# Layer 2's experts: W1 of a slot placed ahead of W2 of the slot before, experts visited in ascending order of tokens, two weight buffers for all of them, and the first slot placed among the sort's matmuls

## The reference, cut to what matters

```python
leaf = zeros(N)
for d in range(4):                       # 16 leaves
    logits = xf @ Wr[off:off+cnt].T + br[off:off+cnt]
    sel = take(logits, leaf);  leaf = leaf * 2 + (sel > 0)
for e in range(16):                      # only the rows of leaf e count
    h = gelu(xf @ W1[e] + b1[e])         # 512 -> 2048
    y = h @ W2[e] + b2[e]                # 2048 -> 512
    out += onehot(leaf)[:, e] * y
x = x + out
```

## Time and profile before

| what | us |
|---|---|
| median of three runs (lowest, highest) | 1835.92 (1829.23, 1841.54) |
| the profiled execution, span; no other time of it is given | 1832.5 |
| PE matmuls busy in the span | 1658.9 (91%) |
| DVE busy | 850.0 (46%) |
| ACT busy | 472.2 (26%) |
| POOL busy | 128.8 (7%) |
| mean granted TensorE clock | 0.942 of full |

### The profile page before, as it was taken

One profiled execution on the slowest core, in us unless ns is written; L12 is line 12 of the kernel. 1 busy time (PEld: TensorE's weight loads), 2 busy tenths in 40 slices (PEclk: granted clock), 3 DMA queues, 4 the chain that ended last, 5 costly groups with the idle time before them and its releaser, 6 DMA issues. The chain is left out here.

```text
span 1832.5 us, 26087 instructions
## 1 busy us (share of the span) xinstructions
PE 1658.9 (91%) x8767; PEld 1029.9 (56%) x8768; DVE 850.0 (46%) x2173; ACT 472.2 (26%) x928; POOL 128.8 (7%) x193
## 2 busy tenths in 40 slices
PE   6889889999999999898999999998899988799964
PEld 3345564476457589896576766656334433464532
DVE  6665376821266674523733426534233322513464
ACT  2012224430020132221636116411223321231220
POOL 0011000000000003431100000001000000200000
PEclk9798999999999899898999989998999989899996
DMA  5131126200071078863000102045998784230000
GB/s 157 63 117 34 43 84 235 80 12 0 10 295 35 25 283 261 272 185 90 4 23 24 72 32 80 1 184 193 427 429 359 300 372 189 83 105 1 0 1 28
DMA packets 69900, 237.69 MB, mean 130 GB/s; under 512 B 14232, under 2 KB 17935, under 8 KB 62913
## 3 DMA queue, kind: packets, MB, share of 16 engines
q1 hardware_dynamic: 54155, 207.34, 30.2%
q0 software_dynamic: 15664, 29.30, 5.4%
HBM read 228.18 MB, written 8.39 MB: 129 GB/s over the span
## 5 line engine op out<-in xcount | busy, mean ns | idle before, releaser
L101 PE MATMUL psum<-ahead_arena 125*125 125x257 f32 (+2 forms) x720 | 218.3, 461 | 4.5 <-DVE ahead_W L2449 3.4
L101 PEld LDWEIGHTS psum<-ahead_arena 125*125 125x125 f32 (+1 forms) x720 | 131.1, 189 | 82.0 <-issue 66.1
L715 DVE TENSOR_SCALAR a0e_ring<-a0e_node,a0e_key 125x625 f16 x198 | 70.2, 388 | 69.8 <-PE psum L520 64.2
L101 PE MATMUL psum<-a_W,1_xn_turned 128*125 128x512 f32 x200 | 91.0, 605 | 1.2 <-DVE a_u L1346 1.2
L518 PE MATMUL psum<-a0e_ring,a0e_tables 125*128 x198 | 74.1, 434 | 18.2 <-DVE a0e_ring L715 10.9
L101 PE MATMUL psum<-a_W,a0l_H 128*125 128x512 f32 x190 | 81.9, 592 | 0.7 <-issue 0.7
L2836 PE MATMUL psum<-ahead_arena,ahead_W 128*32 128x256 f32 x928 | 77.4, 396 | 5.7 <-DMA ahead_arena<-in_L_ffn_W 5.7
L101 PE MATMUL psum<-e_xgT,e_W 128*128 128x156 f32 x512 | 73.0, 306 | 3.0 <-issue 3.0
L101 PEld LDWEIGHTS psum<-e_xgT,e_W 128*128 128x128 f32 x512 | 71.6, 198 | 3.8 <-issue 3.7
L2863 PE MATMUL psum<-ahead_arena,ahead_W 128*32 128x512 f32 x464 | 65.6, 595 | 7.6 <-DMA ahead_arena<-in_L_ffn_W 7.6
L3144 DVE TENSOR_TENSOR ahead_W<-psum,ahead_W 128x256 f32<-128x256 f32 x58 | 24.6, 424 | 97.6 <-PE psum L2849 70.3
(11 more groups left out here) (692 smaller groups left out, 2919.7 us busy)
## 6 DMA issues: line engine op xcount, KB each, us to landing
ahead_arena<-in_L_ffn_W SPq DMA_DIRECT2D x52, 2048.0 KB, 12.6
e_W<-in_L_ffn_W SPq DMA_DIRECT2D x16, 2048.0 KB, 11.0
1_xn_turned<-half_shares SPq DMA_DIRECT2D x16, 256.0 KB, 8.8
a_stage<-in_L_gnn_W SPq DMA_DIRECT2D x8, 512.0 KB, 7.5
ahead_arena<-in_L_gnn_W SPq DMA_DIRECT2D x2, 2048.0 KB, 10.4
a_W<-in_L_gnn_W SPq DMA_DIRECT2D x3, 1024.0 KB, 5.4
a_qkv<-half_shares SPq DMA_DIRECT2D x11, 256.0 KB, 3.3
a_W<-in_L_ffn_w_down POOLq DMA_DIRECT2D x1, 2816.0 KB, 16.2
```

The lines of the kernel that those rows point to most:

```text
L101: last = nc.tensor.matmul(bank[0:rows, at:at + cols], lhs, rhs, start=(n == 0), stop=(n == len(terms) - 1))
L715: nc.vector.tensor_scalar(ring[:, bass.ds(at, 1), 0:NODES].rearrange("p a n -> p (a n)"), node[:, :], key[:, k, bass.ds(t, 1)], None, ALU. ...
```

## The change

PE no longer does a slot from end to end. The order becomes W1 of slot s, W2 of slot s-1, the transposes of slot s; then W1 of slot s+1, and so on. `sums` and `hT` stay single, and so does `xgT`. DVE's order in a slot becomes: copy of the rows, the two bias additions, then the fold of the slot before. ACT has one loop over all slots.

The experts are visited in ascending order of their tokens, expert 0 first. For the first pairs of slots, one from OTHERS alternates with one of the heavy expert. Then the heavy expert's remaining slots follow, and then the remaining experts, which alternate between the two buffers. These always have at least two slots each. The tables are longer (64 entries for slots, 20 for experts), and DVE and PE compute them in more instructions. In its loops DVE reads one register per listed slot.

The heavy expert is named earlier on DVE, and SP's second load no longer waits for the biases. The first slot (expert 0) is worked among the eight sort groups: W1 after the fifth, the transposes after the sixth, W2 after the seventh. The biases are fetched into `c.xn` and added to `x` after the heavy expert's slots. Here is the diff, cut to its core:

```diff
@@ SP
+                    def load(b, e, end):
+                        sync.wait_ge(sem["upper_hidden"], end)
+                        load_wa(sync, b, 0, wa_of(e, 0))
+                        sync.wait_ge(sem["lower_hidden"], end)
+                        load_wa(sync, b, 1, wa_of(e, 1))
+                        sync.wait_ge(sem["summed"], end)
+                        for a in range(2):
+                            load_wb(sync, b, a, wb_of(e, a))
...
-                            sync.wait_ge(sem["bias_fetched"], TILES * 16)
...
+                    with sync.Fori(1, run0 + 1) as v:
+                        first, e = visit_at(sync, v)
+                        load(OTHERS, e, 2 * first)
+                    _, e = visit_at(sync, run0 + 1)
+                    load(HEAVY, e, heavies + pairs + 1)
+                    with sync.Fori(1, couples) as q:
...
@@ PE
+                    def w1(b, s, loaded):
                         pe.wait_ge(wa_landed[b][0], loaded)
                         pe.wait_ge(sem["tokens_ready"], s + 1)
+                        for a, half in enumerate(["upper", "lower"]):
...
+                    def w2_before(b, s, loaded):
+                        pe.wait_ge(sem["y_ready"], s)
+                        for a, half in enumerate(["upper", "lower"]):
+                            pe.wait_ge(wb_landed[b][a], loaded)
+                            pe.wait_ge(sem[half + "_gelu"], s)
...
+                    sort(4)
+                    pe.wait_ge(sem["sorted_freed"], 2)
+                    w1(OTHERS, 0, 16)
+                    pe.wait_ge(sem["places_known"], 1)
+                    sort(5)
+                    pe.wait_ge(sem["sorted_freed"], 4)
+                    turn_hidden(0)
+                    sort(6)
+                    pe.wait_ge(sem["sorted_freed"], 5)
+                    w2_before(OTHERS, 1, 16)
+                    sort(7)
...
-                    nc.tensor.matmul(sums[:, :], c.ident[0:ROWS, :], c.xn[:, 0, :], start=True, stop=True).then_inc(
-                        sem["parts_kept"], 1)
...
+                    w1(HEAVY, 1, 16)
+                    turn_hidden(1)
+                    with pe.Fori(1, pairs) as n:
+                        loaded = visit_of(pe, n) * 16 + 16
+                        w1(OTHERS, 2 * n, loaded)
+                        w2_before(HEAVY, 2 * n, 16)
+                        turn_hidden(2 * n)
+                        w1(HEAVY, 2 * n + 1, 16)
+                        w2_before(OTHERS, 2 * n + 1, loaded)
+                        turn_hidden(2 * n + 1)
+                    with pe.Fori(pairs, heavies) as i:
+                        w1(HEAVY, pairs + i, 16)
+                        w2_before(HEAVY, pairs + i, 16)
+                        turn_hidden(pairs + i)
+                    with pe.Fori(0, couples) as q:
...
+                    w2_before(HEAVY, slots, couples * 16 + 16)
@@ ACT
+                    with act.Fori(1, slots) as s:
+                        nc.scalar.activation(spot[:, 1:2], spot[:, 0:1], ACT.Gelu)
+                        keep_hidden(s)
+                        keep_sums_before(s)
+                        gelus(s)
+                    keep_sums_before(slots)
@@ DVE
+                    def gather(s, place):
                         dve.wait_ge(sem["lower_hidden"], s + 1)
-                        nc.vector.tensor_copy(xgT[:, :, :], xsT[:, :, bass.ds(at, SL)]).then_inc(
+                        nc.vector.tensor_copy(xgT[:, :, :], xsT[:, :, bass.ds(place, SL)]).then_inc(
                             sem["tokens_ready"], 1)
...
+                    def fold_before(s):
+                        dve.wait_ge(sem["parts_kept"], s)
...
+                    def slot(s, place, e):
+                        gather(s, place)
+                        add_bias(s, e)
+                        fold_before(s)
...
+                    with dve.Fori(1, pairs) as n:
+                        place, e = slot_at(dve, n)
+                        slot(2 * n, place, e)
+                        slot(2 * n + 1, heavy_place(n), heavy_e)
+                    with dve.Fori(pairs, heavies) as n:
+                        slot(pairs + n, heavy_place(n), heavy_e)
+                    dve.wait_ge(sem["bias_fetched"], TILES * 16)
+                    for t in range(TILES):
+                        nc.vector.tensor_tensor(c.x[:, t, :], c.x[:, t, :], bias[:, t, :], ALU.add).then_inc(
+                            sem["rows_added"], 1)
+                    dve.wait_ge(sem["rows_added"], TILES)
+                    with dve.Fori(pairs, all_listed) as n:
+                        place, e = slot_at(dve, n)
+                        slot(heavies + n, place, e)
```

More of the change, by code:

```diff
@@ new lines, in w1 @@
+                        for a, half in enumerate(["upper", "lower"]):
+                            if a:
+                                pe.wait_ge(wa_landed[b][1], loaded)
+                            for k in range(CH):
+                                for g in range(QT):
+                                    last = nc.tensor.matmul(
+                                        hid[a][g * SL:(g + 1) * SL, 0:HC], xgT[:, k, :], Wa[b][a][:, k, g, :],
+                                        start=(k == 0), stop=(k == CH - 1))
+                            last.then_inc(sem[half + "_hidden"], 1)
@@ new lines, in _ @@
+                    for v, of in enumerate([eid[:, 0:1], ends[:, 4:5], ends[:, 6:7]]):
+                        nc.tensor.matmul(small[0:1, 132 + RUNS * v:132 + RUNS * (v + 1)], of, of_visit, start=True,
+                                         stop=True)
+                    for v, (of, by) in enumerate([(c.ones[0:EXP2, 0:1], places), (eid[:, 0:1], inside),
+                                                  (before[:, 0:1], inside)]):
+                        last = nc.tensor.matmul(small[0:1, 288 + LIST * v:288 + LIST * (v + 1)], of, by, start=True,
+                                                stop=True)
@@ L3047, in _ @@
                                                 ALU.is_equal).then_inc(sem["moves_made"], 1)
+                    end, heavies, pairs, rem, start, longer, count, rest = [col(ends, n) for n in range(8)]
+                    visit, slot0, token0 = [col(before, n) for n in range(3)]
+                    light_slots = col(V, 2)
                     dve.wait_ge(sem["spread"], 1)
-                    nc.vector.tensor_copy(tot[:, :], small[0:1, 260:266])
-                    nc.vector.tensor_copy(before[:, :], small[0:EXP2, 256:259]).then_inc(done.sem, 1)
@@ new lines, in _ @@
+                    listed_slots, runs_left, run0, half, couples, beyond_v, listed_all, total = [
+                        col(one, n) for n in range(8)]
+                    number, tot_light = tot[0:1, 0:1], tot[0:1, 1:2]
+                    heavies, pairs = heavies[0:1, :], pairs[0:1, :]
+                    numbers = row[0:1, 0:RUNS]
+                    nc.vector.tensor_tensor(listed_slots, tot_light, col(tot2, 1), ALU.add)
+                    nc.vector.tensor_scalar(run0, number, -1.0, col(tot2, 0), ALU.add, ALU.min)
```

600 lines of the change are left out of this document (302 added, 298 removed).

## The result

The changed kernel takes **1908.37 us** (median of four runs, 1898.76 to 1913.51), the kernel before took 1833.99 us in the same rounds (four runs, 1829.23 to 1841.54). The ratio is 1.0406, with a 95% interval of 1.0361 to 1.045: slower by 4.1%. The profiled execution has a span of 1905.1 us, against 1832.5 us, and a mean clock of 0.923 against 0.942.

A forecast was written before the change was run, and what follows sets the result against it. DMA engines (0.78) and clock (0.98) nearly bound the slots together, loads binding the first half. Chain 36.9, clock 32, sort 0 and end 2.5 sum to +71.8 us, giving 1907 us, range 1862 to 1940.

The forecast's parts named there:

- the likeliest case: The slots' chain through DVE plus clock falls in most slots: 1907 us, own range 1888 to 1930, chance 0.55.
- The chain: In each slot, W1 waits for transposes, bias additions, fold and copy in turn: +36.9 us at full clock.
- The clock: In the slots, PE's standstills lower its clock, 1.5 us in eight slots of ten: +32 us.
- a longer low stretch: Rival: in most slots the clock falls for two stretches, about 3 us each: 1956 us, chance 0.11.
- The rival of a steady clock: In the slots the clock holds or falls in a few only: +39 us, 1875 us, chance 0.20.
- The sort and the first slot: Before slot 1, slot 0's gain is taken by the longer table: 0, ends -5 and +4 us.
- The loads: Weight loads in the slots: ordering and buffer reuse help DMA, worth nothing while the chain is longer.
- The end: Behind the last W2, the last fold and stores delay the first fetch: +2.5 us, ends 0 and +4.
- T: The moment in a slot when PE has issued the last matmul of the previous slot's W2.
- The rival "faster": In the slots, fold and copy end before PE finishes W2 and transposes: -34 us, 1802 us, chance 0.05.

The follow-up runs named there:

- e2: The changed kernel with three unread matmuls behind the transposes of every slot but the first, in PE's wait for the copy: 1878.24 us.
- e5: The kernel before with only DVE's copy of the next slot's rows moved behind the fold: 1947.58 us, ratio 1.0608.
- e8: e6 with the light experts in the order of their numbers instead of ascending in tokens: 1857.02 us.
- e12: The changed kernel with only the copy of rows moved ahead of the bias additions and fold of the slot before: 1805.51 us, ratio 0.986.
- e7: e6 with the copy of a slot's rows moved ahead of the bias additions of the slot before: 1802.89 us, ratio 0.9835.
- e1: The changed kernel with the fold moved behind the next copy of rows and ahead of the bias additions: 1831.55 us, ratio 0.9984.
- e3: The changed kernel with one add in the fold instead of three, so it computes less than the reference: 1843.12 us.
- e6: e1 with the output bias fetches moved ahead of the last store and its additions behind the last fold: 1819.92 us, ratio 0.9931.
- e11: e7 with the five output bias fetches issued behind the stores of three late slots, not ahead of the last store: 1790.64 us, ratio 0.9764.

## Why the prediction was right, point by point

The forecast was 1907 us and the measurement 1908.37 us; the likeliest case, the chain with falls of the clock in most slots, was the one that came about. Its signs are there: the copy right behind the fold, 27 waits of 3.7 us on average, no wait for loads, a DMA share of 0.62 and a clock of 0.86 over the whole stretch. That the two numbers agree to 1.4 us is luck: the chain was put 6 us too high, the clock 9 us too low and the end 2.5 us too high, and these cancel; the four runs alone lie up to 10 us from their median.

**The chain.** Its links are where they were predicted: transposes, two additions, three adds of the fold, the copy, W1, with 3.13 us of standing still in a pair (3.2 predicted). The 26 intervals from slot 2 to slot 28 were put at 302.9 us at full clock. By e2's periods they are 7 x 10.81 + 6 x 11.28 + 10.60 + 14.84 + 11 x 11.47 = 295.0 us. About half of the error is the register read: taken at 0.8 us more than in a pair, it cost 11.28 - 10.82 = 0.46 between pairs and 11.46 - 10.82 = 0.64 in the listed slots. The lower bound (0.5, against 0.1 in a pair) was the better value. Most of the rest is a period inside a pair of 10.81 instead of 10.95 us, an error that every interval shares. The first interval was 10.0 us instead of 8.4, as ACT was late once and PE waited 1.97 us for it. The last slot took 16.2 instead of 14.3, with W2 at the low clock. Without the fall in that W2, 5.34 - 3.62 = 1.7 us, it is 14.5. At full clock the stretch is 10.0 + 295.0 + 14.5 = 319.5 us: the chain costs +31 us, not +36.9.

**The clock.** The same 26 intervals took 334.5 us in the changed kernel (1300.79 to 1635.33): 39.5 us more than at full clock, or 1.5 us per interval, where I took 1.2. The number of falls was slightly overestimated, eight slots in ten against 19 of 27: 17 of 19 behind gaps of 3.58 us and more, and 2 of 7 behind 3.13 to 3.15 us. What was too low is the price of one, 1.5 us. In 11 slots W1 took 5.35 to 5.41 us instead of 3.66, or 1.7 us more, but in 8 it took 6.0 to 6.4 us, or 2.3 to 2.8 us more; the mean of the 19 is 2.1 us. The prediction had a longer low stretch only as a rival, in most slots and at 3 us. With the last slot the clock cost 41 us, not 32. e2 agrees: it gives back 30.1 us while it has a wait of its own of 10.6 us for the first store and two slow W1. The rival of a steady clock (1875 us) is ruled out by it.

By the rule of the Trainium skill's page "TensorE: Matmul & The Clock Gate", section "Loop structure matters more than you think", which the prediction weighed, results copied out by VectorE would have cost nothing in clock; e2 and e5 show that this does not carry over to a loop in which the next matmuls wait for VectorE instead of following at once. Nearer to this case is that page's section "A second HAM failure mode: psum-queue depth-cycling", in which short idles between groups of matmuls, repeated each iteration, make the clock go up and down. That page's case is in bf16; the traces here, in 32-bit floats, agree: behind 19 of 27 waits W1 ran slow, each W2 behind it was at full clock again (3.61 or 3.62 us), and the mean clock is 0.85 with the gaps and 0.97 with them filled.

**The sort and the first slot.** Predicted 0. The block starts 4.9 us later in this trace, in unchanged code ahead of it; counted from there, W1 of slot 1 comes at 1285.9 us, against 1286.45 before. Right in the sum. Its two halves, what slot 0 gains and what the longer table takes, were not measured apart in the changed kernel.

**The loads.** "Real for DMA, and worth nothing as long as the chain above is longer" was nearly right: the second buffer is worth at most 12.6 us under the chain, 5.2 of them seen as waits for weights, and 32.8 us without it. What the prediction did not see is that the ascending order has a worth of its own, the four padded slots of e8. It counted that there is no padding, but not that the order is the reason.

**The end.** Predicted +2.5 us. The first gather starts 1653.21 - 1651.54 = 1.7 us behind the last W2, against 1.0 before: +0.7. With T at 1642.35, where the transposes of the last slot start, the fetch comes at T + 10.9, as predicted; the last W2 ended later than predicted, as it took 5.34 us at the low clock, which is counted above. The first long matmuls of layer 3 start 20.0 us behind the last W2 before (1595.15) and 20.1 us behind it after (1671.60), so the end costs nothing.

**The other side.** The rival "faster" named its own condition, fold and copy done before PE is through with W2 and the transposes, and priced it at 1802 us with pairs at 19.7 and the rest at 7.7 us per slot. The condition was not met by the change; e12 takes the copy out from behind the fold and takes 1805.5 us, and e7 shows 7.61 us per listed slot. The price was near, but not in each part: e12's stretch is 261.2 us instead of 254.4, with 12.0 us of the first store's wait, which the price did not have. My expectation for e1 used that price without its condition, as there the bias additions still stand ahead of the copy, and missed by 30 us.

## What to carry to other kernels

When matmuls are reordered so that a stage overlaps the one before, write down for each other engine the order of its queue, and ask of every instruction that feeds the next matmul what stands ahead of it; here one copy of 0.23 us, left behind 2.9 us of work that TensorE did not need yet, turned a gain of 28 us into a loss of 74. The gaps are 99 us in all; what the chain adds to the slots is 31 us net, and the clock behind the gaps another 41, so price the two together. And a store that a fold waits for should not be queued behind fetches that are needed only much later.

## What the runs showed of the hardware

- The length of a gap alone did not settle whether the clock falls. Behind 2.99 us it fell in nearly every slot of e5, behind 3.13 us only in 2 of 7 in the changed kernel, behind 3.80 us not in the last W1 of the changed kernel, and behind 1.82 to 1.84 us in 5 of 11 in e3, while none of the last twelve slots of e6 had a slow W1, behind waits of 1.58 to 1.76 us. In e11, two waits for weights of the same length, 20 us apart, had different ends (W1's half behind the wait, and W2 behind it):

```profile
1368.60 2.56 PE L2857 MATMUL psum<-ahead_arena,ahead_W 128*32 128x256 f32 x32 [2.76 <-DMA ahead_arena<-in_L_ffn_W]
1370.91 4.75 PE L2878 MATMUL psum<-ahead_arena,ahead_W 128*32 128x512 f32 x32
...
1388.46 1.93 PE L2857 MATMUL psum<-ahead_arena,ahead_W 128*32 128x256 f32 x32 [2.73 <-DMA ahead_arena<-in_L_ffn_W]
1390.21 3.62 PE L2878 MATMUL psum<-ahead_arena,ahead_W 128*32 128x512 f32 x32
```

- A store of 64 KB that is issued behind five indirect fetches, at a DMA share of 0.89, released its waiter 19.3 us after its issue (e1, 1298.85 to 1318.18), and in e6, which fetches late, no wait for it is left; at the end of the slots, at a DMA share of 0.09, the step from the last store to the gather behind it took 3 us (changed kernel, 1650.26 to 1653.21).
- Three unread matmuls per slot, 2.74 us of PE's time each slot, saved 30 us in all.
